# One tile of rows in every fourth block fetched row by row by SyncE, and three waits of TensorE removed, in a graph attention layer with a routed FFN

## What is computed

```python
xp = (layernorm(x) @ W).reshape(n, H, C)
alpha = leaky_relu(a_src[src] + a_dst[dst])       # one number per edge and head
ex = exp(alpha - amax[dst])
agg = segment_sum(xp[src] * (ex / denom[dst]), dst)
x = x + elu(agg + bias)
```

## Time and profile before

| | us |
|---|---|
| median of 3 runs | 2186.64 |
| profiled execution | 2193.97 |
| its span, first to last instruction | 2192.2 |
| TensorE matmul busy | 1883.2 (86%) |
| VectorE busy | 1533.1 (70%) |
| ScalarE busy | 1154.9 (53%) |
| GpSimd busy | 1525.6 (70%) |

### The profile page before, as it was taken

How to read it: one execution, slowest core, us unless ns; L and a number is a source line. 1 busy time by engine, 2 the same in 40 slices (tenths; PEclk the granted TensorE clock), 3 DMA queues, 4 the chain that set the end, 5 groups by cost and what they waited for, 6 DMA issues and landing times.

```text
span 2192.2 us, 29093 instructions
## 1 busy us (share of the span) xinstructions
PE 1883.2 (86%) x9507; PEld 1547.8 (71%) x9508; DVE 1533.1 (70%) x3416; ACT 1154.9 (53%) x1672; POOL 1525.6 (70%) x1626
## 2 busy tenths in 40 slices
PE   8945888898899889888888888889889889888887
PEld 6734777777677777777777776767677777777775
DVE  5556776677677667767767777777667667777776
ACT  4543555555555555555555555555555555555533
POOL 2367777777777777777777777777777777777710
PEclk9977999999999999999999999999999999999988
DMA  8854455455455555554555555455545545555457
GB/s 281 296 167 136 134 145 146 133 146 146 136 142 146 146 137 142 146 141 133 146 146 137 142 146 146 138 140 147 146 132 145 146 135 142 144 147 138 135 226 284
DMA packets 157136, 340.11 MB, mean 155 GB/s; under 512 B 46645, under 2 KB 73937, under 8 KB 155698
## 3 DMA queue, kind: packets, MB, share of 16 engines
q0 software_dynamic: 75088, 208.19, 35.0%
q1 hardware_dynamic: 74706, 116.59, 16.7%
q10 hardware_dynamic: 7184, 13.41, 1.6%
HBM read 299.38 MB, written 38.68 MB: 154 GB/s over the span
## 4 chain that ended last, share of the span: by engine, by line
POOL 49%; issue 22%; PE 12%; DMA 11%; ACT 3%; DVE 1%; POOLq 1%; DVEq 0%; SPq 0%; ACTq 0%
POOL rows L710 49%; DMA rows<-node_rows,ends 10%; PE ag_ps L972 4%; ACT rows L854 3%; PE ag_ps L1097 2%; PE y_ps L1080 2%; PE h_ps L1061 2%; POOLq L410 1%; PE ag_ps L1168 1%; PE ag_ps L1169 0%; DVE rows L1443 0%; DMA steps_of_rows<-in_L_gnn_att_dst 0%; DMA selfr<-in_dst,edge_block 0%; PE xl_ps L1001 0%; PE tr_ps L1001 0%
## 5 line engine op out<-in xcount | busy, mean ns | idle before, releaser
L710 POOL DMA_INDIRECT rows<-node_rows,ends x1563 | 1484.1, 950 | 493.2 <-issue 449.9
L1097 PE MATMUL ag_ps<-rows,oh 128*128 128x260 f32 x3518 | 835.4, 398 | 26.1 <-DVE rows L1443 25.6
L1097 PEld LDWEIGHTS ag_ps<-rows,oh 128*128 128x128 f32 x3518 | 690.3, 200 | 172.6 <-DVE rows L1443 51.8
L1061 PE MATMUL h_ps<-xnT,w1s 128*128 128x256 f32 x1568 | 457.1, 443 | 215.9 <-DVE zz L1424 201.1
L1443 DVE TENSOR_TENSOR rows<-rows,xl_ps 128x512 f32<-128x512 f32 (+3 forms) x392 | 503.1, 1346 | 47.2 <-ACT rows L874 47.2
L1061 PEld LDWEIGHTS h_ps<-xnT,w1s 128*128 128x128 f32 x1568 | 327.7, 217 | 291.6 <-DVE zz L1424 209.8
L1080 PE MATMUL y_ps<-w2s,hT 128*128 128x256 f32 x1568 | 368.8, 384 | 11.5 <-DVE oh L1405 7.6
L1080 PEld LDWEIGHTS y_ps<-w2s,hT 128*128 128x128 f32 x1568 | 296.2, 191 | 71.6 <-DVE oh L1405 25.9
L1424 DVE TENSOR_TENSOR zz<-rows,edge_dm 128x72 f32<-128x72 f32 x98 | 22.8, 233 | 447.8 <-DMA rows<-node_rows,ends 432.7
L854 ACT COPY rows<-rows 128x780 f32<-128x780 f32 x97 | 81.6, 842 | 403.5 <-DMA rows<-node_rows,ends 403.5
L1405 DVE TENSOR_TENSOR oh<-xl_ps,dloc 128x2304 f32<-128x2304 f32 x98 | 249.0, 2541 | 0.0
(11 more groups left out here) (245 smaller groups left out, 1528.9 us busy)
## 6 DMA issues: line engine op xcount, KB each, us to landing
spare<-dst SPq DMA_DIRECT2D x97, 288.0 KB, 4.7
rows<-node_rows,ends POOLq DMA_INDIRECT x1563, 2.9
selfr<-node_rows SPq DMA_DIRECT2D x98, 130.0 KB, 3.0
base<-in_x SPq DMA_DIRECT2D x14, 896.0 KB, 7.0
base<-in_x SPq DMA_DIRECT2D x49, 256.0 KB, 3.3
ffn_rows<-yb ACTq DMA_DIRECT2D x48, 256.0 KB, 4.8
node_rows<-base SPq DMA_DIRECT2D x13, 910.0 KB, 5.5
base<-in_x_turned SPq DMA_DIRECT2D x14, 384.0 KB, 7.5
```

Of the source, the lines that this page charges most:

```text
L710: pool.indirect_dma_start(out=rows[:, b, t, :], out_offset=None, in_=table, in_offset=bass.IndirectOffsetOnAxis(ap=ends[:, b, t, 0:1], axi ...
L1061: last = nc.tensor.matmul(h_ps[:, m * PAIR:(m + 1) * PAIR], w1s[:, c, n * P:(n + 1) * P], xnT[:, c, :], start=(c == 0), stop=(c == DC - 1))
L1097: product = nc.tensor.matmul(ag_ps[b][:, 0:ROW], oh[:, b, t, :], rows[:, b, t, :], start=(t == 0), stop=False)
```

## The change

One tile (number 9) of blocks 6, 10, 14, ..., 94 is no longer gathered by GpSimd. SyncE loads the 128 source numbers of that tile into one partition, reads them eight at a time into registers, and issues one DMA for each row, 32 rows in each of the four blocks ahead, into a buffer of its own (`stage`, two in turn). ScalarE copies the buffer into `rows` (`move_staged`) ahead of `carry`, and VectorE's zz waits for the copy. The waits on `gath` count one tile less in such a block (`given`, `given_up_to`). On TensorE the three waits named above go. Five semaphores are dropped or shared to make room for the new ones (`minus_ok`, `ex_ok`, `selfx_ok`, `d16_st` and `win_st`); ScalarE's first wait becomes one for `loc_ok`, a step of VectorE soon after the earlier one. The diff, cut to its core:

```diff
+    STAGED, EVERY, FIRST_STAGED = 9, 4, 6
+    staged_blocks = [w for w in range(FIRST_STAGED, NW - 1) if (w - FIRST_STAGED) % EVERY == 0]
+    ROWS_A_TURN = P // EVERY
+    AT_ONCE = 8
+    def given(w):
+        return TILES - 3 - (w in staged_blocks) if w < NW - 1 else LAST - 3
+    def given_up_to(w):
+        return sum(given(v) for v in range(w % 2, w + 1, 2))
...
+        stage = [xrow[:, :], spare[:, 5 * D:5 * D + ROW]]
+        sources = [xoh[0:1, :].bitcast(I32), spare[0:1, 5 * D + ROW:5 * D + ROW + P].bitcast(I32)]
...
                 sp.dma_start(selfr[:, b, :], table[bass.ds(w * P, P), :]).then_inc(ld_self[b], 16)
+                if sp_extras is None:
+                    stage_rows(w)
...
+            def stage_rows(w):
+                n, turn = divmod(w + EVERY - FIRST_STAGED, EVERY)
+                if n >= len(staged_blocks) or w + EVERY < FIRST_STAGED:
+                    return
+                k = n % 2
+                if turn == 0:
+                    if n == 0:
+                        sp.wait_ge(parts_ok, 1)
+                    tile = in_edges(entry(sp, staged_blocks[n], 0, NCH - TILES) + STAGED)
+                    with nc.allow_non_contiguous_dma("the sources of a tile's edges to one partition"):
+                        sp.dma_start(sources[k], edges[:, bass.ds(tile, 1), 0].rearrange("p t -> t p")).then_inc(src_ld, 16)
+                    if n >= 2:
+                        sp.wait_ge(moved, n - 1)
+                    sp.wait_ge(src_ld, 16 * (n + 1))
+                for at in range(turn * ROWS_A_TURN, (turn + 1) * ROWS_A_TURN, AT_ONCE):
+                    _, nodes_of = nc.values_load_multi_w_load_instructions(
+                        sources[k][:, at:at + AT_ONCE], engines=[mybir.EngineType.SP], min_val=0, max_val=NW * P - 1,
...
+                    for j, node in enumerate(nodes_of):
+                        sp.dma_start(stage[k][at + j:at + j + 1, :], table[bass.ds(node, 1), :]).then_inc(row_ld[k], 16)
...
-                    gather(t, gath[b])
+                    if not (pool_extras is None and w in staged_blocks and t == STAGED):
+                        gather(t, gath[b])
...
+            def move_staged(w, b):
+                n = staged_blocks.index(w)
+                act.wait_ge(row_ld[n % 2], 16 * P * (n // 2 + 1))
+                act.wait_ge(freed[GROUPS - 1], w - 1)
+                nc.scalar.copy(rows[:, b, STAGED, :], stage[n % 2]).then_inc(moved, 1)
...
-                    if isinstance(w, int):
-                        pe.wait_ge(zs_ok, w + 1)
                     hidden(w - 4, b, i - 2, (1,))
...
                     ffn_out(w - 4, b, i - 2, (0,))
-                    if isinstance(w, int) and w + 1 < NW:
-                        pe.wait_ge(oh_ok, w + 2)
                     ffn_out(w - 4, b, i - 2, (1,))
                 if known(w, 3) and not (isinstance(w, int) and w == NW - 2):
-                    if isinstance(w, int) and w + 2 < NW:
-                        pe.wait_ge(dm_ok, w + 2)
                     hidden(w - 3, 1 - b, i - 2 + b, (0,))
...
+                    dve.wait_ge(gath[b], 16 * given_up_to(w))
+                    if w in staged_blocks:
+                        dve.wait_ge(moved, staged_blocks.index(w) + 1)
```

More of the change, by code:

```diff
@@ L239, in build @@
         ROOMS = len(yin)
+        stage = [xrow[:, :], spare[:, 5 * D:5 * D + ROW]]
+        sources = [xoh[0:1, :].bitcast(I32), spare[0:1, 5 * D + ROW:5 * D + ROW + P].bitcast(I32)]
+        assert FLAT // 2 + 4 <= 5 * D and 5 * D + ROW + P <= 7 * D
         chunks = []
@@ L315, in sems @@
             return [sem(n) for n in names.split()]
-        dst_ld, att_ld, b2_ld, w_ld, d16_st, edge_ld, win_st, win_ld = sems(
-            "dst_ld att_ld b2_ld w_ld d16_st edge_ld win_st win_ld")
+        dst_ld, att_ld, b2_ld, w_ld, edge_ld, side_st, win_ld = sems(
+            "dst_ld att_ld b2_ld w_ld edge_ld side_st win_ld")
         x_ld, tab_st = [sem(f"x_ld{q}") for q in range(DEEP)], sem2("tab_st")
@@ L349, in build @@
         y_ld = [sem(f"y_ld{k}") for k in range(ROOMS)]
+        src_ld, row_ld, moved = sem("src_ld"), sem2("row_ld"), sem("moved")
         def bc(v, n):
@@ L493, in batch_io @@
                     sp.wait_ge(d16_ok, 1)
-                    sp.dma_start(dst8_dram.rearrange("(p e) -> p e", p=P), dst8).then_inc(d16_st, 16)
+                    sp.dma_start(dst8_dram.rearrange("(p e) -> p e", p=P), dst8).then_inc(side_st, 16)
             def first_edge(w):
@@ L514, in _ @@
             sp.wait_ge(win_ok, 1)
-            sp.dma_start(win_dram, wi[0:NW, :]).then_inc(win_st, 16)
-            sp.wait_ge(win_st, 16)
+            sp.dma_start(win_dram, wi[0:NW, :]).then_inc(side_st, 16)
+            sp.wait_ge(side_st, 32)
             sp.dma_start(win[:, :], win_dram.rearrange("(a w) c -> a (w c)", a=1)).then_inc(win_ld, 16)
@@ L523, in _ @@
             store_rows(NB - 1, 1, BATCH - EDGE, EDGE)
-            sp.wait_ge(d16_st, 16)
             load_targets(0, 0, first)
@@ L549, in window @@
                 sp.dma_start(selfr[:, b, :], table[bass.ds(w * P, P), :]).then_inc(ld_self[b], 16)
+                if sp_extras is None:
+                    stage_rows(w)
                 if known(w, 1):
                     extra_loads(w - 1)
+            def stage_rows(w):
[15 more added lines that the diff above has]
+                        sources[k][:, at:at + AT_ONCE], engines=[mybir.EngineType.SP], min_val=0, max_val=NW * P - 1,
+                        skip_runtime_bounds_check_because="an edge's source is one of the nodes")
+                    for j, node in enumerate(nodes_of):
+                        sp.dma_start(stage[k][at + j:at + j + 1, :], table[bass.ds(node, 1), :]).then_inc(row_ld[k], 16)
             def extra_loads(w):
@@ L847, in store @@
                 act.dma_start(by_partition(y_dram, 2 * p, 2), yb[:, :, :]).then_inc(y_st, 16)
+            def move_staged(w, b):
[3 more added lines that the diff above has]
+                nc.scalar.copy(rows[:, b, STAGED, :], stage[n % 2]).then_inc(moved, 1)
             def carry(w, i, b):
-                act.wait_ge(gath[b], 16 * (TILES - 3) * (i + 1))
+                if act_extras is None:
+                    act.wait_ge(gath[b], 16 * given_up_to(w))
+                else:
+                    act.wait_ge(gath[b], 16 * (TILES - 3) * (i + 1))
                 if known(w, 1):
@@ L866, in exponentials @@
             def exponentials(w, i, b):
+                if act_extras is None and w in staged_blocks:
+                    move_staged(w, b)
                 if not isinstance(w, int) or w < NW - 1:
@@ L923, in _ @@
             nc.scalar.preload_act_table_set(EXP_AND_LN)
-            act.wait_ge(minus_ok, 1)
+            act.wait_ge(loc_ok, 1)
             for w in range(2):
@@ L1421, in exponents @@
                 dve.wait_ge(dm_ok, w + 1)
-                dve.wait_ge(gath[b], 16 * ((TILES - 3) * i + n - 3))
+                if dve_extras is None:
+                    dve.wait_ge(gath[b], 16 * given_up_to(w))
+                    if w in staged_blocks:
+                        dve.wait_ge(moved, staged_blocks.index(w) + 1)
+                else:
+                    dve.wait_ge(gath[b], 16 * ((TILES - 3) * i + n - 3))
                 dve.wait_ge(gath_last[b], dve.to_reg(optional_landed(dve, w)))
```

14 lines of the change are left out of this document (7 added, 7 removed).

## The result

The changed kernel takes 2201.34 us (median of 8 runs, 2190.04 to 2212.45), the kernel before 2186.51 beside it (8 runs, 2182.31 to 2191.46): ratio 1.0073, 95% interval 1.0055 to 1.0092. It is 0.7% slower; the forecast was 1.5% faster, 2154.8 us. The time lies inside the range, on the side of rival B.

A forecast was written before the change was run, and what follows sets the result against it. GpSimd's row gathers were taken as the bound, at 20.08 us a block. Gains of 28.8 us (fewer gathers) and 3 us (waits removed), with SyncE's work hidden, make 31.8: median 2186.64 becomes 2154.8 us, range 2147 to 2262.

The forecast's parts named there:

- rival B: SyncE becomes the bound: a row over 0.465 us delays ends until GpSimd waits; 2425 us at 0.56 a row; chance 27%.
- part 2: SyncE's added issues: 18.3 us a block against a period of 19.78, so hidden with 1.5 us to spare.
- 32 rows: SyncE's one-row DMAs in each block: 0.42 us each start to start, bounds 0.28 to 0.62.
- 4 register loads: SyncE's loads of eight addresses before every 8 rows: 0.5 us each, upper bound 4 us.
- source numbers: SyncE's issue, load and landing wait once in four blocks: 3.9 us, or 1.0 a block.
- the old issues: SyncE's four issues and a register load from before the change: 1.9 us a block.
- the point given for failure: On SyncE, forecast wrong if a row exceeds 0.465 us start to start or eight values take over 1.0 us to load.
- Part 1: GpSimd issues 23 gathers fewer at 1.25 us each: 28.8 us gained, mean period 19.78 us.
- The slack of TensorE: At GpSimd's holds by TensorE, 1.5 us left at least in a staged block, so GpSimd keeps its pace.
- Part 3: TensorE without three waits: idle moves into one stretch before the sums; 3 us gained, at most 9 lost or 6.9 gained.
- rival A: TensorE's single long idle lowers its clock in nearly every block, costing 9 us: 2166.8 us profiled; chance 9%.
- ScalarE's copy: Copy of the staged tile, near 372 ns, hidden by 4.23 us of idle; 9 us if that cover were gone.

The follow-up runs named there:

- loads16: The changed kernel with 16 values in a register load instead of 8, two loads a block, not four: 2168.44 us, ratio 0.9921.
- sources_early: The changed kernel with the next staged tile's source numbers loaded two blocks ahead: 2167.06 us, ratio 0.9918.
- early_waits: The changed kernel with source numbers loaded two blocks ahead and TensorE's three waits put back: 2160.95 us, ratio 0.9886; run again 2159.76 us, 0.9884.
- rows_only: The changed kernel with TensorE's three waits put back: 2207.35 us, ratio 1.0105.
- half_rows: The changed kernel with 64 rows one by one, 16 a block, and one plain DMA of 64 fixed (wrong) rows for the others: 2171.2 us, ratio 0.9944.
- every8: The changed kernel with a staged tile in every eighth block, 11 in all, and 16 rows a block: 2181.8 us, ratio 0.9987.

## Why the prediction was wrong

**The step that failed** is the sum of part 2, "32 x 0.42 + 4 x 0.5 + 1.0 + 1.9 = 18.3 us, against 19.78: hidden, with 1.5 us to spare". It came out at 20.46:

| term | forecast | measured | from |
|---|---|---|---|
| 32 rows | 13.4 | 13.4 | 0.42 start to start |
| 4 register loads | 2.0 | 3.3 | three behind rows, 0.79 and some 0.06 around it: (15.79 - 0.22 - 28 x 0.42) / 3 - 0.42 = 0.85; the first, 0.53, is 0.75 with what is around it |
| source numbers | 1.0 | 1.5 | (25.3 - 19.3) / 4, 19.3 being the block with base<-in_x (1007.12 to 1026.42) |
| the old issues | 1.9 | 2.3 | 19.06, the mean of 18.82 and 19.3, less the rows and loads |

The sum of the right column is 20.5. The term that got the argument and the bounds, the price of a row, was right; the register load, taken at the one-value gap of the earlier trace rows because "for eight values I take 0.5 too", was short by 1.3 us a block, and this alone nearly used up the 1.5. The load itself is 0.53 for the first of a block, as in the forecast, but 0.75 with what stands around it; the three behind rows take 0.79 and 0.85, a place for which the forecast had no row. The source numbers' landing (3 us taken between 2.0 and 9.7) and the old issues added 0.9. `loads16` and `sources_early` show that either of the first two decides. So the point given for failure was too far off: "if eight values take more than 1.0 us to load, too" looked at each term with the others held at their guess, when 0.78 sufficed together with the others. Rival B had the right mechanism and the wrong trigger (a row over 0.465 us). With 20.46 its own formula, 92 x (20.46 - 20.08) - 12, gives 23 us lost; 15 were measured, and in the execution that the 20.46 is from only 3.5 (2190.04 against 2186.51). So the lead that is used up first was more than the 12 us, and the first long wait for ends, at 1009.87 with 43 of 98 zz done, shows the same. That the time lies in the range is not to the sum's credit: the upper part of the range was made for dearer rows, which did not come.

**Part 1**, 28.8 us, was right as a price (x1540, 1.25 us apart) and right as a gain once SyncE is out of the way: `early_waits` has 23 and 26 of them (2184.19 to 2160.95, 2185.77 to 2159.76). The slack of TensorE, "1.5 us left at least", did not hold in every block: holds were 18.9 to 29.5 us in the versions with fewer gathers and no waits that GpSimd paces, and up to 26.1 with the waits.

**Part 3** was forecast as a gain of 3 us within -9 to +6.9. It loses 2.2 us in the kernel before and 5 to 9 us where GpSimd's period is shorter (each pair on two chips). The forecast saw what would happen (the slow clock moves onto the sums) and rated its gain, the FFN part done before zz, above its price. That is rival A's condition, the low clock on the sums: it exists, and taking it away is worth up to its price of 9 us, though not all of that is seen in the holds that A named; it did not set this result. In the kernel bound by SyncE the sign may be the other (changed kernel 1.0073, `rows_only` 1.0105, on different chips, intervals of 1.0055 to 1.0092 and 1.0090 to 1.0121 that just touch); this stays open.

**ScalarE's copy** was forecast as hidden. In 16 of the 23 blocks nothing is seen to wait for it; in 7 VectorE's zz waits for it:

```profile
DVE zz L1476 <- ACT rows L895: 26.4, 7, 4.5
```

In the first of these (zz at 1071.82) the copy's own rows had been issued by 1061.04, but ScalarE had stood still for the targets until 1066.40 and had two one-hot steps (4.3 us) to do before the copy at 1070.67. So the copy was late through the targets' load behind SyncE's rows. With the source numbers early the list has no such wait.

## What to carry to other kernels

An engine that waits for 1717 of 2192 us can be filled to its limit by one helper job, and the sum that decides has many small terms: when the margin is under a tenth of the period, give each term its bounds and add the bounds up, the cheap-looking ones (register loads, a stand-still for an address) first, and take the price of each where it will stand, rather than spend the care on the largest. A wait for data that an in-order queue itself asked for a moment earlier was cheap to remove here (34 us for one moved load): ask two blocks ahead. And before waits are taken out, look on which work the slow clock falls afterwards: here idle just ahead of the products that free GpSimd's buffers cost 5 to 9 us more than idle ahead of products that nobody waited for.

## What the runs showed of the hardware

- A DMA of one 1 KB row into one partition, at an address from a register: 0.22 us on SyncE, 0.42 from start to start with its two register operations; DMAs into 128 partitions take 0.34 to 0.43 by themselves (medians of L504 before, L528, L561 and L565).
- A register load of 8 values took 0.53 us as the first of a block and 0.79 right behind eight one-row DMAs, in the changed kernel as in `half_rows` and `every8` with two loads a block. For 16 values it was 0.98 and 1.24 (`loads16`). Whether the rows ahead of it are the cause was not separated.
- 128 numbers of 4 bytes, each a piece of its own, into one partition: 0.57 us to issue, then 3.8 us of waiting (79 us in 21 places), 6.1 from the issue to the next row, register load included.
- The ends' load, 2.0 us to landing before, took 4.2 right behind 32 rows in the queue; with 16 rows a block, and SyncE waiting for zz in between, it is 2.0 again (`half_rows`, `every8`). The changed kernel in the profile's DMA issues (count, KB each, median us to landing):

```profile
ends<-in_edges SPq DMA_DIRECT2D x97, 18.0 KB, 4.2
```
